# Flamingo block on one core: weight clamps moved to GpSimd, a third-order root step, six landing places, a new order of work

## The reference

```python
x = x + jnp.tanh(g_xattn[0]) * _L0_xattn_ref(4, 256, 256, w, u, _layernorm(x), ctx)     # WKV scan along the tokens
x = x + jnp.tanh(g_ffn[0])   * _L0_ffn_ref(_layernorm(x), w_gate, w_up, w_down)         # ternary weights, 8-bit tokens
x = x + jnp.tanh(g_xattn[1]) * _L1_xattn_ref(_layernorm(x), ctx, Wq, Wk, Wv)            # 32 heads of width 8, RMS-normed q and k
x = x + jnp.tanh(g_ffn[1])   * _L1_ffn_ref(_layernorm(x), gate_w, gu_w, dp_w, ...)      # 64 experts, top 8, and one shared
```

## Time and profile before

| what | us |
|---|---|
| median of three runs (478.32 to 481.01) | 480.92 |
| the profiled execution | 480.34 |
| its span, first to last instruction | 478.6 |
| busy: TensorE, VectorE, ScalarE | 399.1, 379.5, 302.0 |

### The profile page before, as it was taken

One profiled execution on the slowest core, in us unless ns is written; L12 is line 12 of the kernel. 1 busy time (PEld: TensorE's weight loads), 2 busy tenths in 40 slices (PEclk: granted clock), 3 DMA queues, 4 the chain that ended last, 5 costly groups with the idle time before them and its releaser, 6 DMA issues.

```text
span 478.6 us, 7806 instructions
## 1 busy us (share of the span) xinstructions
PE 399.1 (83%) x2612; PEld 193.7 (40%) x2612; DVE 379.5 (79%) x817; ACT 302.0 (63%) x442; POOL 0.2 (0%) x4
## 2 busy tenths in 40 slices
PE   1011966697776897999999999999999999999996
PEld 1010444342424454554534443554444444444443
DVE  5999499999998869999797898897456666777754
ACT  5896686689696766757898677464234444444422
POOL 0000000000000000000000000000000000000000
PEclk9999999577898899999999999999999999999999
DMA  8500200000002164114425336244222655556511
GB/s 295 223 1 0 66 1 1 1 1 0 2 2 66 46 213 128 56 57 121 140 72 159 119 111 195 80 143 131 87 66 73 209 164 167 167 172 175 174 38 44
DMA packets 31506, 47.47 MB, mean 99 GB/s; under 512 B 5610, under 2 KB 15210, under 8 KB 30956
## 3 DMA queue, kind: packets, MB, share of 16 engines
q1 hardware_dynamic: 31468, 46.98, 31.4%
HBM read 45.65 MB, written 1.31 MB: 98 GB/s over the span
## 4 chain that ended last, share of the span: by engine, by line
PE 61%; DVE 22%; ACT 7%; issue 4%; DMA 3%; SPq 2%; DVEq 0%; ACTq 0%
PE ps L1593 31%; PE ps L1927 15%; PE ps L1702 5%; PE ps L1690 2%; DVE xn L1034 1%; DVE bn L1015 1%; DMA regC<-in_ctxT_dram 1%; DVE rep L1163 1%; DVE regW L1483 1%; PE ps L1618 1%; DMA regP<-in_dp_dram 1%; PE ps L1584 1%; ACT exs L723 1%; SPq L538 1%; PE ps L1712 1%
## 5 line engine op out<-in xcount | busy, mean ns | idle before, releaser
L934 ACT ACTIVATE regW<-ps 128x512 f32<-128x512 f32 x51 | 30.4, 597 | 92.6 <-PE ps L1593 89.7
L1593 PE MATMUL ps<-hH,regC 128*128 128x512 f16 x264 | 85.8, 380 | 0.1
L1500 DVE TENSOR_TENSOR regW<-ps,regW 128x512 f32<-128x512 f32 x64 | 44.1, 690 | 51.8 <-PE ps L1593 49.0
L1593 PE MATMUL ps<-hH,regW 128*128 128x512 f16 x248 | 80.9, 383 | 0.2 <-DVE regW L1500 0.2
L1593 PE MATMUL ps<-hL,regC 128*128 128x512 f16 x132 | 50.0, 379 | 0.0
L1927 PE MATMUL ps<-regW,regC 128*128 128x512 f16 x198 | 48.1, 379 | 0.0
L1593 PE MATMUL ps<-hL,regW 128*128 128x512 f16 x124 | 47.4, 382 | 0.0
L1927 PE MATMUL ps<-regW 128*128 128x512 f16 x180 | 43.8, 379 | 3.4 <-DVE regW L1483 3.4
L1483 DVE TENSOR_TENSOR regW<-regW 128x512 f16<-128x512 f32 x64 | 43.6, 681 | 0.1
L947 ACT CAST regW<-regW 128x512 f16<-128x512 f32 x64 | 39.2, 612 | 0.6 <-DVE regW L1521 0.5
L1593 PEld LDWEIGHTS ps<-hH,regC 128*128 128x128 f16 x264 | 25.8, 98 | 32.6 <-issue 3.6
(11 more groups left out here) (202 smaller groups left out, 662.1 us busy)
## 6 DMA issues: line engine op xcount, KB each, us to landing
regW<-routing_dram SPq DMA_DIRECT2D x130, 128.0 KB, 3.1
regP<-in_gu_dram SPq DMA_DIRECT2D x56, 256.0 KB, 2.6
regP<-in_dp_dram SPq DMA_DIRECT2D x56, 128.0 KB, 2.7
regO<-in_ffn_dram SPq DMA_DIRECT2D x3, 1024.0 KB, 9.4
x<-in_x_dram SPq DMA_DIRECT2D x2, 512.0 KB, 8.3
regC<-in_ctxT_dram SPq DMA_DIRECT2D x1, 1024.0 KB, 5.3
regP<-in_proj_dram SPq DMA_DIRECT2D x1, 768.0 KB, 12.2
out_dram<-x SPq DMA_DIRECT2D x1, 512.0 KB, 3.5
```

The source lines that it names most:

```text
L934: nc.scalar.activation(sgm[:, c % 2, :], bank(gate_bank(c)), ACT.Silu, scale=UNSCALE).then_inc(esilu_done, 1)
L1500: V.tensor_tensor(rows, bank(gate_bank(c) + 1), rows, ALU.mult).then_inc(et_done, 1)
L1593: mm = T.matmul(out_ap, w(k), a(k), start=(n == 0), stop=(n == 3 * DK - 1))
```

## The change

- `ternary_weights` becomes a GpSimd program: two passes for each third, the second one waiting for the first. `clamp_from_below` is gone.
- `bits_root` does one step of third order (four instructions) and one Newton step (three) in place of three Newton steps.
- Landing places: the two in `regP` and four in `fw`, free once the network of half 1 is through (`down_done`). Entries below 11 use the first two. Seven entries, not five, are issued before `store_routing(0)`; entries 11 to 14 go to `fw` at chunks 9 and 10 of SyncE's loop, later ones five chunks after the entry that they replace was split.
- All lists and tables are ordered anew, with other PSUM banks. In the prologue: `high_projections`, `low_part(1)` and `low_part(2)` stand before the quotients, `project(0)` before `turn_y(0)` and the network's products, `row_sums(0)` before `norm(1)`; `turned_rows(2)` and `(3)`, `running_max(2)` and `clamps(2)` before `norm(4)`; `weights_high` and `weights_low` of entries 0 to 6 (before: 0 to 4) ahead of chunk 0. `wide_silu` and `wide_inner` of tile 4 move from ahead of chunk 0 into it, and the network of half 1 runs some chunks later.

```diff
-        mst = regP[:, :].rearrange("p (b n) -> p b n", b=NS)
+        mst = [cut(regP, PW * i, PW) for i in range(NS)]
...
+        mst += [fw[:, 2 * PW * i:2 * PW * (i + 1)].bitcast(F32) for i in range(4)]
...
+        MORE = 11
+        STAGE = [e % NS if e < MORE else (2, 3, 4, 5, 1, 0)[(e - MORE) % 6] for e in range(ENTRIES)]
+        FORMER_THERE = [max((f for f in range(e) if STAGE[f] == STAGE[e]), default=None) for e in range(ENTRIES)]
...
+        AHEAD = NS + EARLY + 2
         LOAD_IN = {}
-        for e in range(NS + EARLY, ENTRIES):
-            LOAD_IN[SPLIT_AT[e - NS] + 3] = e
+        for e in range(AHEAD, ENTRIES):
+            if e < MORE:
+                at = SPLIT_AT[FORMER_THERE[e]] + 3
+            elif FORMER_THERE[e] is None:
+                at = 9 + (e - MORE) // 2
+            else:
+                at = SPLIT_AT[FORMER_THERE[e]] + 5
+            LOAD_IN.setdefault(at, []).append(e)
...
         BESIDE_SCALAR = {
-            (0, "A"): [("turned_weights", 0, 1), ("wide_silu", 5, 0, 4), ("ffn_scale", 4), ("wide_silu", 5, 1, 6)],
-            (1, "A"): [("ffn_turned", 4, 4), ("ffn_scale", 5), ("wide_silu", 6, 0, 6)],
-            (2, "A"): [("weights_high", 5), ("weights_high", 6), ("wide_silu", 6, 1, 6)],
+            (0, "A"): [("wide_silu", 4, 0, 4), ("turned_weights", 0, 1), ("wide_silu", 4, 1, 6)],
+            (1, "A"): [("wide_silu", 5, 0, 4), ("ffn_scale", 4)],
+            (2, "A"): [("wide_silu", 5, 1, 6), ("wide_silu", 6, 0, 4)],
...
         BESIDE_VECTOR = {
-            (0, "A"): [("wide_inner", 5, 0, 5), ("wide_inner", 5, 1, 7)],
-            (1, "A"): [("wide_inner", 6, 0, 7)],
-            (1, "B"): [("ffn_residual", 4, 5)],
-            (2, "A"): [("weights_low", 5), ("wide_inner", 6, 1, 7)],
+            (0, "A"): [("wide_inner", 4, 0, 5), ("wide_inner", 4, 1, 7), ("wide_inner", 5, 0, 5)],
+            (1, "C"): [("wide_inner", 5, 1, 7)],
...
         BESIDE_PRODUCTS = {
-            (0, "B"): [("turn_weights", 0, 1), ("wide_products", 5, 0, 4)],
-            (1, "A"): [("wide_products", 5, 1, 6)],
-            (1, "B"): [("turn_hidden", 4, 4)],
-            (2, "A"): [("wide_products", 6, 0, 6), ("narrow", 4, 5)],
+            (0, "B"): [("turn_weights", 0, 1)],
+            (1, "B"): [("wide_products", 5, 0, 4)],
+            (2, "A"): [("wide_products", 5, 1, 6), ("wide_products", 6, 0, 4)],
...
             def load_entry(e):
-                if e >= NS:
-                    sp.wait_ge(mwH_ready, e - NS + 1)
-                    sp.wait_ge(mwL_ready, e - NS + 1)
+                f = FORMER_THERE[e]
+                if f is not None:
+                    sp.wait_ge(mwH_ready, f + 1)
+                    sp.wait_ge(mwL_ready, f + 1)
+                if e == MORE:
+                    sp.wait_ge(down_done, TT)
...
-            for e in range(NS + EARLY):
+            for e in range(AHEAD):
                 load_entry(e)
             store_routing(0)
...
-                for i in range(3):
-                    link(V.scalar_tensor_tensor(t, r, -0.5, v, ALU.mult, ALU.mult))
-                    link(V.tensor_tensor(t, t, r, ALU.mult))
-                    link(V.scalar_tensor_tensor(r, t, 1.5, r, ALU.add, ALU.mult))
+                link(V.tensor_tensor(t, v, r, ALU.mult))
+                link(V.tensor_tensor(t, t, r, ALU.mult))
+                link(V.scalar_tensor_tensor(t, t, -10.0 / 3.0, t, ALU.add, ALU.mult))
+                link(V.scalar_tensor_tensor(r, t, 5.0, r, ALU.add, ALU.mult))
+                k = 3.0 / 8.0
+                link(V.scalar_tensor_tensor(t, r, -0.5 * k ** 3, v, ALU.mult, ALU.mult))
+                link(V.tensor_tensor(t, t, r, ALU.mult))
+                link(V.scalar_tensor_tensor(r, t, 1.5 * k, r, ALU.add, ALU.mult))
...
+        @block.gpsimd
+        def _(pool):
+            def ternary_weights(m):
+
+                w = fw[:, 2048 * m:2048 * (m + 1)]
+                pool.wait_ge(fz_ready, m + 1)
+                nc.gpsimd.tensor_scalar(w, fst[m], -MAGIC, 1.0, ALU.add, ALU.min).then_inc(fcut, 1)
+                pool.wait_ge(fcut, m + 1)
+                nc.gpsimd.tensor_scalar(w, w, -1.0, None, ALU.max).then_inc(fw_ready, 1)
```

More of the change, by code:

```diff
@@ new lines, in bass_flamingo @@
+            (3, "C"): [("weights_low", 7), ("weights_low", 8), ("ffn_residual", 4, 5), ("wide_inner", 7, 0, 7)],
+            (4, "C"): [("wide_inner", 7, 1, 5), ("weights_low", 9), ("ffn_residual", 5, 7), ("stats", 8),
+                ("norm", 8)],
+            (5, "C"): [("low_halves", 8, 4), ("ffn_residual", 6, 5), ("weights_low", 10), ("ffn_residual", 7, 7),
+                ("stats", 9), ("row_sums", 5), ("rows", 5)],
+            (6, "C"): [("split_low", 10), ("split_low", 11), ("norm", 9)],
@@ new lines, in bass_flamingo @@
+            (6, "A"): [("narrow", 7, 7), ("project", 5, 6), ("project", 6, 4)],
+            (7, "C"): [("turn_rows", 10, 7), ("turn_rows", 11, 6)],
+            (8, "A"): [("turn_norm", 9, 7)],
+            (8, "B"): [("scores", 32, 4)],
+            (10, "A"): [("scores", 33, 6)],
+            (10, "C"): [("scores", 34, 4)],
+            (11, "A"): [("weighted_values", 16, 7), ("scores", 35, 4), ("project", 7, 6)],
+            (11, "B"): [("scores", 36, 4), ("weighted_values", 17, 7), ("turn_rows", 12, 6)],
@@ L463, in bass_flamingo @@
+            (20, "B"): [("weighted_values", 30, 7)],
+            (20, "C"): [("weighted_values", 31, 6)],
+            (21, "B"): [("heads_out", 6, 4), ("heads_out", 7, 6)],
+            (23, "C"): [("turn_norm", 11, 7)],
+            (24, "C"): [("logits", 1, 7)],
+            (26, "C"): [("turn_weights", 1, 7)],
         }
@@ L783, in _ @@
             to_integers(1)
-            clamp_from_below(1)
             to_integers(2)
-            high_projections()
+            project(0, 4)
             norm_root(1)
@@ L1761, in _ @@
-            narrow(2, 7)
-            turn_hidden(3, 4)
-            turn_norm(2, 7)
-            narrow(3, 6)
-            project(1, 5)
-            project(2, 2)
+            turn_y(0, 6)
+            turn_norm(1, 2)
+            gate_product(0, 4)
+            up_product(0, 6)
+            gate_product(1, 4)
+            gate_product(2, 2)
+            up_product(1, 0)
+            gate_product(3, 4)
+            up_product(2, 6)
+            turn_hidden(0, 2)
+            up_product(3, 4)
@@ L1767, in _ @@
+            turn_hidden(1, 0)
+            narrow(0, 3)
+            turn_hidden(2, 6)
+            narrow(1, 2)
+            narrow(2, 5)
+            turn_hidden(3, 6)
+            turn_norm(2, 5)
+            narrow(3, 7)
+            project(1, 6)
+            project(2, 4)
+            turn_rows(0, 6)
+            turn_rows(1, 3)
             turn_norm(3, 4)
-            turn_rows(0, 7)
-            turn_rows(1, 1)
-            turn_rows(2, 0)
-            turn_rows(3, 7)
+            turn_rows(2, 6)
@@ L1795, in _ @@
+            scores(9, 0)
+            scores(10, 2)
+            scores(11, 0)
+            weighted_values(4, 6)
+            scores(12, 2)
+            turn_rows(4, 7)
+            project(3, 5)
+            weighted_values(5, 7)
             scores(13, 2)
-            scores(14, 4)
-            weighted_values(5, 6)
-            scores(15, 0)
+            scores(14, 0)
+            scores(15, 4)
+            turn_rows(5, 6)
+            project(4, 6)
             weighted_values(6, 3)
-            weighted_values(7, 2)
@@ L1819, in _ @@
+            turn_y(1, 6)
+            turn_rows(6, 4)
+            turn_rows(7, 3)
+            heads_out(0, 0)
+            heads_out(1, 4)
+            scores(16, 2)
+            scores(17, 6)
+            scores(18, 0)
+            scores(19, 2)
+            scores(20, 6)
+            weighted_values(8, 5)
+            scores(21, 0)
+            scores(22, 2)
+            weighted_values(9, 4)
+            scores(23, 6)
+            scores(24, 0)
+            weighted_values(10, 5)
             scores(25, 2)
+            turn_norm(5, 4)
```

582 lines of the change are left out of this document (254 added, 328 removed).

## The result

| | us |
|---|---|
| before, median of 4 runs beside it (478.3 to 481.9) | 480.97 |
| changed, median of 4 runs (507.0 to 509.4) | 508.42 |
| ratio, 95% interval | 1.058 [1.055, 1.061] |
| span of the profiled execution (478.6 before) | 507.5 |

The account below looks back on a forecast made before the run. VectorE was taken to bound the prologue and TensorE the experts' stretch; -2.6 + 1.7 - 0.5 - 1.5 - 1.6 + 0.2 = -4.3 took 480.3 to 476.0 us, range 472 to 485.

Parts of the forecast that it names:

- The upper bound for one pass: GpSimd clamps in the prologue: one pass takes between 1.22 and 4.6 us, with 2.1 taken.
- Rival A: Prologue: GpSimd and VectorE hold each other up, 483.8 whole; chances 0.15 in part, 0.06 whole, 0.12 with long passes.
- Rival C: Prologue: GpSimd clean but slow, above 4.2 us a pass, delaying `up_product(0)`; 477.6 at 4.6; chance 0.20 together with rival B.
- The gain up to the first `ffn_inner` (-2.6): Prologue: `rqs` 0.8 us earlier and products sooner behind it, so `ffn_inner(0)` at 52.8 against 55.44.
- Attention (+1.7 - 0.5 - 1.5 = -0.3): Attention: two more `weights_low` before `norm(7)` +1.7 us, shorter root of `rows(4)` -0.5, fewer VectorE waits -1.5.
- The term for `rows(4)`: Attention: its bit root has ten steps for twelve, 0.26 us apart, -0.5 us.
- Landing places (-1.6 + 0.2): Experts' stretch: earlier loads of entries 5 and 6 cut TensorE's waits from 4.7 to 3.1 us; `turned_weights` waits 0.2 more.
- what is late next?: Experts' stretch, after the transfer wait goes: VectorE's `product(1)` behind the weighting of chunk 0, TensorE waiting 1.6 us.
- rival B: Experts' stretch and attention: transfer was hidden anyway, order only moves waits; -1.2, 479.1; chance 0.20 together with Rival C.
- Covered by TensorE: Experts' stretch: the seven other bit roots lie under TensorE's work, so shortening them is worth nothing.
- D: Attention and experts' stretch: all waits go but TensorE's 1.1 us; 473.5, or 472.3 with earliest `ffn_inner(0)`; chance 0.12.
- A in part: Prologue: VectorE slips through half of GpSimd's gaps, about 480 us (478 to 482); chance 0.15.

Follow-up runs that it names:

- a3: Changed kernel with the clamps back on VectorE, the second and third third behind `token_scales(0)`, no GpSimd program: 480.3 us, ratio 1.001.
- a4: a3 plus the six GpSimd passes, written to memory that nobody reads and awaited only in the attention: 511.9 us (one run).
- b5: Kernel before with a test ahead of it: GpSimd passes alone, then single VectorE instructions during passes; a pass took 7.1 us with two operations, 5.4 with one.
- c1: Changed kernel with the accumulator form of `tensor_scalar` in `norm(1)`, for its times alone: 499.6 us (one run).
- d2: a3 with eight entries ahead of the routing store and 32 and 6 unread products in TensorE's idle stretch: 475.2 us, ratio 0.991.
- d1: Kernel before with only the new root step (one of third order, one Newton step): 478.6 us, ratio 0.997.
- b2: a3 with eight entries, not seven, issued ahead of the routing store: 478.45 us, ratio 0.996.
- b3: a3 with three Newton steps in place of the third-order step and one Newton step: 483.7 us, ratio 1.007.
- a1: Kernel before with only the six clamping passes moved to GpSimd: 508.4 us, ratio 1.062.
- d3: b2 with `project(0)` back behind `turn_norm(1)`, as in the kernel before: 478.6 us, ratio 0.997.

## Why the prediction was wrong

*The clamps on GpSimd: the step that failed.* The upper bound for one pass, 4.6 us, was twice a VectorE pass, and the value taken, 2.1, was ScalarE's. Another engine's row bounds nothing for GpSimd: it takes 5.4 and 7.1. Rival A had the right mechanism, that the two engines hold each other up until all six passes have ended, and the right rate: "6 us more" for each us of a pass. With the mean pass of 37.6 / 6 = 6.3 us its own sum is 483.8 + 4.2 x 6 = 509, and 508.4 was measured. That this agrees so closely is in part luck: its base, 476.0, was 4.3 too low (a3 takes 480.3), and the instructions that stood longest were not those that it named. The text stopped at d = 4 and gave long passes 0.12, and its range ended at 485. Rival C needed GpSimd clean, and a4 shows that it isn't.

*Which instructions are contested.* That "the normalizing and the reductions have at most one SBUF tensor in" was given as evidence against A. For the reductions it holds; the four normalizing instructions are 18.19 us for 1.38, most of the loss. In the changed trace and in b5 plain `tensor_scalar` is held to the end of the pass, and in c1 the accumulator form isn't. The Trainium skill (SBUF — State Buffer, "Who interferes with whom") says this: `tensor_scalar` can enter a mode that uses both port pairs, "not the form that also writes out its accumulator", and then excludes GpSimd for a whole instruction. The prediction cited that section for the two-input rule and left the other half of it out. For two inputs the same page (section "SBUF: two separate sides") says a whole instruction too; there the measurement differs, 2.8 and 3.37 us where the rest of the pass was 5.4.

*The price on the page.* The Trainium skill (GPSIMD Engine Reference, section 3.1) has 1.03 cycles an element, some 1.8 us by estimate. At the 1.2 GHz of that page the measured 7.08 us for 2048 elements are 4.1 cycles, and 5.37 are 3.1. The measurement decides.

*The gain up to the first `ffn_inner` (-2.6).* It had two parts, 0.8 ahead of `rqs` and 1.8 behind. In a3 `rqs` is at 46.54, 0.4 later than before, where the forecast's steps with 1.9 us of clamps still ahead of it give 1.1 later; so the part ahead of `rqs` was no loss. From `rqs` to `ffn_inner` the forecast had 7.3 us. The kernel before takes 9.3, a3 and the changed kernel 8.1, d2 6.4. The difference between a3 and d2 is the clock: TensorE, idle for 8.5 us, does the network's first products at half speed, for which the text had "0.22 to 0.43 each, by the clock" and took a value between. The early `project(0)` takes away the work that had raised the clock for the products.

*Attention (+1.7 - 0.5 - 1.5 = -0.3).* Measured -0.4 in the changed kernel as a whole. Since this stretch differs by 2.4 us between before and d1, of which the root is 0.5, that agreement shows little. The term for `rows(4)` is confirmed (0.52 in d1); the other two were not measured apart.

*Landing places (-1.6 + 0.2).* The wait for entries 5 and 6 went, and the wait on `product(1)` came with 1.4 us for the forecast 1.6. What failed is "what is late next?": it was asked of VectorE and not of SyncE. Entry 7 is in the old place of entry 6, the first issue behind the store; it costs 1.7 on TensorE, 1.5 in all (b2). Even with that mended, b2 takes 320.4 us from `logits(0)` to the end, as before, and not 1.4 less: what the waits give back is lost again, which is rival B's outcome for this stretch. The later entries were costed rightly at nothing, but their landing places also gained nothing: ScalarE's waits for a landing behind `logits(0)` fell from 14.5 us to 2.6 in the changed kernel, and all but the first were waits that TensorE never felt.

*"Covered by TensorE."* The seven roots were costed at nothing because TensorE is busy 259.5 of 260 us. That table is an average over 260 us. In the new order VectorE is busy 94% of the time from 186 to 236 us and without a gap around one of the roots, and at each of the seven roots two instructions more cost their own length. It is 2.8 us in favour of the change (b3), so without the new root step the change would cost 3 us even with the clamps on VectorE. Why this order has less room there than the old one stays open. From `logits(0)` to the end a3 takes 1.6 us more than before, and TensorE's busy time there is 1.0 us more (311.67 for 310.65) with the same products.

*What is left of the sum.* From a3's 480.3 the medians go to 478.45 with the eighth entry (b2) and to 475.2 with the filled idle stretch (d2). By stretches, in us against the kernel before:

| stretch | forecast | a3 | d2 |
|---|---|---|---|
| start to first `ffn_inner` | -2.6 | -0.8 | -2.7 |
| from there to `logits(0)` | -0.3 | -0.7 | -2.5 |
| from there to the end | -1.4 | +1.6 | -0.2 |

For a3 the forecast's first entry is -0.7, with the 1.9 us of clamps that stay. So what a3 lacks is in the experts' stretch, 3.0 us; 1.5 of them are entry 7 and the rest is open. That d2 comes out at the forecast's 476 is in part luck: its attention gained 2.5 where 0.3 was forecast, by a clock that varies from one execution to the next, and the experts' 1.4 never came.

*The chances.* The text gave 0.40 to "faster". Its own parts make 0.30 (half of 0.35, and D's 0.12): the times that it names for B, C and A in part all lie above the bound of 476.1, so the rest had nothing to stand on.

## To carry to other kernels

Before moving work to an engine that the trace shows idle, find a row of that engine on such a tile, or treat its price as unbounded and ask what then stands; and ask of each instruction on the neighbour's path, by its form and not by its number of inputs, whether the two exclude each other. Where a transfer's wait is removed, look at the queue for what is now the first issue behind the same obstacle. Work moved out of an idle stretch of TensorE ahead of a product chain also takes away what raised its clock, and an engine at 99% in a table of 260 us hides stretches in which another engine sets the pace. And before a difference of 1 or 2 us between two traces is given a cause, look at how much one kernel differs from execution to execution: here by 5 us, with the granted clock.

## What the runs showed of the hardware

- GpSimd's `tensor_scalar` on 128 x 2048: 7.08 us with two operations, 5.37 with one, whatever the types; 128 x 1024 with two 3.64; a `memset` of 128 x 2048 f32 1.80.
- While such a pass runs, plain `tensor_scalar` from SBUF to SBUF on VectorE stands until it ends, with 4 columns too. In a run of four (changed kernel, a1) the first three each stood until the end of a pass: GpSimd's next pass began within 0.1 us of the end of the one before. The other way round, one GpSimd pass took 6.21 us for 5.36 when a VectorE clamp of 2048 columns got into the gap ahead of it (a4).
- `tensor_tensor` with both inputs in SBUF was let through 4.3 to 4.6 us into the pass of 7.1, at all four meetings of the changed kernel and b5 (34.95, 48.03; 60.86, 103.98: start plus length, less its own length, less the start of the pass), and 3.5 us into a pass of 5.4 in a4 (56.29). `tensor_reduce`, `bn_stats`, operations with an input in PSUM, and the accumulator form of `tensor_scalar` ran at their own length.
- TensorE's granted clock was 0.50 (1.2 GHz) in the network's products of a3 after 8.5 us without work, and 1.00 (2.4 GHz) in d2, which filled them. In the attention, with the same steps, it averaged 0.89 from 106 to 136 us in a3 and 1.00 in d2 and d3, and the way from `ffn_inner` to `logits(0)` took 1.7 us less in d2. What sets it there wasn't found. It differs between executions of one kernel: the mean over the whole was 0.957 to 0.977 in the kernel before, with 482 and 477 us.
